# Projections by seven block products from the second group on, with weight operands fetched by ScalarE's queue

## The chip, the cores and the metric

One core of a Trainium2 chip runs the kernel. The metric is the device time in microseconds of one execution. Engine names are those of the profile: PE (TensorE), PEld (its weight loads), DVE (VectorE), ACT (ScalarE), POOL (GpSimd), and SP, whose queue issues every DMA of the kernel before.

## What is computed

The input x is 4 x 2048 x 512 (batch, rows, channels), in float32. The first half of the block is causal attention with one head of width 512; the second half, a gated sparse feed-forward layer, is not touched by the change.

```python
h = layernorm(x)
q = relu(h @ Wq + bq)
k = relu(h @ Wk + bk)
v = relu(h @ Wv + bv)
e = q @ k.T / sqrt(512) - 10000 * causal
attn = softmax(e)
x = x + layernorm(relu((attn @ v) @ Wo + bo))
x = x + layernorm(ffn(layernorm(x)))
```

## The kernel before, in words

**Precision.** Every float32 operand of an attention matmul is held as two float16 parts, high and low. A product is three matmuls (high by high, high by low, low by high), written by `three` (line 628), each with its own load of a 128 x 128 weight. The high part is an ACT activation, the low part a DVE or POOL subtraction after it.

**Stages.** The 8192 rows are 16 groups of 512 rows (g = 0 to 15), four groups to a batch; a group has four tiles of 128 rows. The attention phase runs over half steps H = 8g + h. `stages` (line 79) gives the half steps h = 0, 1 to v, 2, 3 to q, 4, 5 to k, each with two blocks of 128 output channels, and 6, 7 to v times Wo. `project` (line 642) makes one block: 4 channel chunks by 3 matmuls with 512 moving columns, so 48 matmuls for each of v, q and k of a group. Between them stands the attention of the group before: scores of a tile in h = 0, 2, 4 (and of the group's own first tile in h = 7), attention by values in h = 1, 3, 5, 6. `pe_items` (line 117) writes the order: in h = 0 and 1 the projection comes first, in the others attention does. A score tile at position t of its batch has t/4 + 1 chunks of up to 512 columns, so the attention work of a group grows fourfold along a batch. The group in which the attention of a batch begins (g = 1, 5, 9, 13; `opening`) is the shortest.

**Banks.** Six PSUM banks are one ring for projections, v times Wo and scores (`m_items`, line 278; `take_m`, line 635): a matmul group waits for the release of the bank six items before. Two more banks take attention by values.

**Evacuation.** `relu` (line 886, ACT) reads a finished block twice, as float32 `raw` and as the float16 high part; `lo_vqk` (line 1168, DVE) makes the low part. The order of each engine is written by hand in one loop over H per engine: SP line 557, PE 710, ACT 941, DVE 1355, POOL 1690. Each queue is strictly in order. What DVE does in an opening group, in its order:

- h = 0: low parts of v, residual statistics of an earlier tile, `score_rows` (line 1191), `convolution` (line 1270: one normalisation, two products, two reductions)
- h = 1: low parts of v and of the probabilities (`lo_p`), `convolution`, two `ln_stats` of the next group's rows (line 1156)
- h = 2: `score_rows`, low parts of q and probabilities, `bias_o` (line 1227), four `ln_norm` (line 1163)
- h = 3, 5: statistics or `convolution`, low parts, `bias_o`; h = 4: `score_rows`, low parts, statistics
- h = 6, 7: the low parts of v times Wo between the same kinds of work; two more `ln_stats` at the end of h = 7

**Rows of the next group.** SP loads them (`load_x`, line 457) at h = 5, two groups ahead; DVE normalises them in h = 2; ACT (`hi_h`, line 881) and POOL (`lo_h`, line 1648) split them in h = 3; SP transposes eight pieces of 128 x 512 by DMA into `hT`, double buffered (`transpose_h`, line 464).

**Start.** The four weight matrices are loaded into `w_stage` (line 381, the memory of v), split by `weight_hi` (line 871, ACT) and `weight_lo` (line 1144, DVE), and stay in SBUF for the whole phase. POOL's `ln_scale` (line 1638) waits for `ln_stats` of all four tiles of a group.

## Time and profile before

| | |
|---|---|
| median of 3 runs | 2062.92 us (2062.69 to 2063.83) |
| the profiled execution | 2062.52 us |
| its span | 2060.4 us |
| attention phase, in the trace | about 0 to 1390 us |
| granted clock of TensorE, mean | 0.998 |

The span is from the first to the last instruction of the program; the 2.1 us between it and the execution's time lie around it. In the page a busy share is that of the whole span. In a timeline the bracket holds the idle time of the engine before the row and who ended it. A row of a window gives the stretch, its length, then for PE, PEld, DVE, ACT and POOL the busy time and in brackets the instructions that run in it, then the granted clock, the DMA share and GB/s.

### The profile page before, as it was taken

The page shows a single profiled execution, that of the slowest core. Times are in us where ns is not written, and L with a number is a line of the kernel's source. Part 1 is how long each engine was busy: PE and PEld are TensorE (multiplying, and loading weights), DVE is VectorE, ACT ScalarE, POOL GpSimd, SP SyncE. Part 2 cuts the span into 40 slices and gives each one's busy share as a digit, 9 for nine tenths or more (in the row PEclk, how much of TensorE's full clock was granted, in tenths as well). Part 3 has the DMA queues.
Part 4 walks back from the last instruction along what each step waited for, and adds up shares of the span by engine and source line. Part 5 has one row for each costly group of instructions (what it writes and reads, how often), then busy time and mean ns, then how long its engine had stood idle before and what let it go on. Part 6 is the DMA issues. An engine that isn't in the chain of part 4 may idle for free. (4 is left out here: it accounts for less than half of the span.)

```text
span 2060.4 us, 30926 instructions
## 1 busy us (share of the span) xinstructions
PE 2002.2 (97%) x9419; PEld 937.9 (46%) x9419; DVE 1520.3 (74%) x3285; ACT 1101.9 (53%) x2268; POOL 1108.7 (54%) x1304
## 2 busy tenths in 40 slices
PE   8999999999999999999999999998999999999997
PEld 4444444444444444444444444453444444444443
DVE  6576554677555467565547765579999999999999
ACT  5444433344333434443334443335888888888885
POOL 2243322354323245333225432325999999999997
PEclk9999999999999999999999999999999999999999
DMA  5234342344342334423343332261222223223221
GB/s 185 75 92 112 73 99 73 99 110 110 86 102 76 78 90 125 102 77 95 78 94 97 110 88 66 88 179 63 80 96 93 88 87 98 94 96 97 89 78 67
DMA packets 301593, 194.85 MB, mean 95 GB/s; under 512 B 223858, under 2 KB 241394, under 8 KB 301428
## 3 DMA queue, kind: packets, MB, share of 16 engines
q1 hardware_dynamic: 301428, 192.88, 33.7%
q8 instruction: 75, 1.23, 0.3%
q14 instruction: 90, 0.74, 0.1%
HBM read 82.69 MB, written 58.72 MB: 69 GB/s over the span
## 5 line engine op out<-in xcount | busy, mean ns | idle before, releaser
L631 PE MATMUL psum<-hT,w_hi 128*128 128x512 f16 (+1 forms) x1544 | 458.3, 379 | 0.0
L631 PE MATMUL psum<-kT,qT 128*128 128x512 f16 (+3 forms) x1920 | 363.4, 347 | 1.5 <-DVE kT L1173 1.5
L631 PE MATMUL psum<-v,pT 128*128 128x512 f16 x1632 | 362.5, 379 | 0.7 <-DMA pT<-phl 0.7
L631 PE MATMUL psum<-hT,w_lo 128*128 128x512 f16 (+1 forms) x772 | 292.3, 379 | 0.0
L631 PEld LDWEIGHTS psum<-kT,qT 128*128 128x128 f16 x1920 | 180.9, 98 | 184.1 <-issue 2.9
L905 ACT ACTIVATE sS<-sS,nm 128x128 f32<-128x128 f32 (+7 forms) x64 | 76.9, 1201 | 345.9 <-DVE nm L1216 345.8
L894 ACT ACTIVATE raw<-psum,bqkv_s 128x512 f32<-128x512 f32 x192 | 131.2, 683 | 218.7 <-PE psum L631 216.5
L631 PEld LDWEIGHTS psum<-v,pT 128*128 128x128 f16 x1632 | 159.7, 98 | 193.1 <-issue 1.2
L1528 DVE MAX8 c<-cut 128x8 f32<-128x512 f32 x384 | 247.0, 691 | 0.0
L631 PEld LDWEIGHTS psum<-hT,w_hi 128*128 128x128 f16 x1544 | 151.5, 98 | 176.2 <-DVE w_lo L1147 0.3
L1655 POOL TENSOR_SCALAR ve<-mv 128x1 f32<-128x1 f32 x64 | 22.5, 352 | 348.2 <-DVE mv L1242 347.3
L631 PE MATMUL psum<-fw,xsT 128*128 128x512 f16 x768 | 176.2, 379 | 0.7 <-ACT xsT L1053 0.7
L631 PE MATMUL psum<-fw,h2T 128*128 128x512 f16 x768 | 176.5, 379 | 0.0
L1524 DVE MATCH_REPLACE8 cut<-c,cut 128x512 f32<-128x512 f32 x256 | 172.6, 688 | 0.0
L1730 POOL TENSOR_TENSOR sel<-ex,rest 128x512 f32<-128x512 f32 x126 | 160.7, 1275 | 11.6 <-DVE rest L1524 11.6
L1665 POOL TENSOR_TENSOR xr<-ob,xr 128x512 f32<-128x512 f32 x62 | 78.7, 1269 | 160.0 <-ACT ob L924 160.0
L631 PE MATMUL psum<-w_hi,vT 128*128 128x512 f16 x512 | 158.2, 379 | 0.0
L1205 DVE TENSOR_SCALAR_CACHE_REDUCE sS<-psum 128x512 f32<-128x512 f32 x96 | 66.0, 690 | 115.9 <-PE psum L631 115.6
L790 PE MATMUL psum<-lw,xa 128*128 128x512 f32 x252 | 142.7, 648 | 0.0
L1642 POOL TENSOR_SCALAR ve<-mv 128x4 f32<-128x4 f32 (+1 forms) x19 | 5.7, 302 | 228.4 <-DVE mv L1161 228.3
L1173 DVE TENSOR_TENSOR qT<-raw,qT 128x512 f16<-128x512 f32 x64 | 47.0, 735 | 102.3 <-ACT qT L895 102.3
L1178 DVE SCALAR_TENSOR_TENSOR v<-psum,v 128x512 f16<-128x512 f32 x64 | 44.0, 687 | 102.0 <-ACT v L900 102.0
(177 smaller groups left out, 3754.2 us busy)
## 6 DMA issues: line engine op xcount, KB each, us to landing
xg<-x SPq DMA_DIRECT2D x64, 256.0 KB, 5.1
xr<-x SPq DMA_DIRECT2D x64, 256.0 KB, 2.9
h_scratch<-hb SPq DMA_DIRECT2D x64, 256.0 KB, 3.0
h<-h_scratch SPq DMA_DIRECT2D x64, 256.0 KB, 2.7
x<-x_scratch SPq DMA_DIRECT2D x64, 256.0 KB, 3.0
x_scratch<-xr SPq DMA_DIRECT2D x62, 256.0 KB, 2.0
out<-zn SPq DMA_DIRECT2D x59, 256.0 KB, 2.0
xcg<-xc_scratch SPq DMA_DIRECT2D x16, 512.0 KB, 4.1
```

The source lines that it names most:

```text
L631: mm = nc.tensor.matmul(outp, stat(a), mov(c), start=(n == 0 and k == 0), stop=(n == total - 1 and k == 2))
L790: nc.tensor.matmul(L_BANK[s], xa[:, slot, j, s, :], lw[:, s, :], start=False, stop=True).then_inc(lg_ps.sem, 1)
L894: nc.scalar.activation(raw[:, n % 2, :], bank, ACT.Relu, bias=bias, scale=QKV_DOWN)
L905: nc.scalar.activation(sS[:, T % 2, 0:w], sS[:, T % 2, 0:w], ACT.Exp, bias=nm[:, T % 3:T % 3 + 1], accum_out=ssum[:, T % 3:T % 3 + 1]).the ...
L1173: nc.vector.tensor_tensor(dst[:, 1], raw[:, n % 2, :], dst[:, 0], ALU.subtract).then_inc(vqk_lo.sem, 1)
L1178: nc.vector.scalar_tensor_tensor(v[:, 1, T % TILES, :], m_bank(("vo", g, j)), V_DOWN, v[:, 0, T % TILES, :], ALU.mult, ALU.subtract).then_ ...
L1205: nc.vector.tensor_scalar(dst, src, S_SCALE, None, ALU.mult, ALU.max, accum_out=pm[:, T % 3, j:j + 1]).then_inc(s_ev.sem, 1)
L1524: nc.vector.match_replace(dst, eight, src, 0.0).then_inc(top_ok.sem, 1)
L1528: nc.vector.max(dst, src).then_inc(top_ok.sem, 1)
L1655: nc.gpsimd.tensor_scalar(ve2[:], m[:, 1:2], EPS * O_GAIN * O_GAIN, None, ALU.add).then_inc(ve2_ok.sem, 1)
L1665: nc.gpsimd.tensor_tensor(xr[:, T % 4, :], ob[:, T % 2, :], xr[:, T % 4, :], ALU.add).then_inc(x1_ok.sem, 1)
L1730: nc.gpsimd.tensor_tensor(sel[:, k % 2, s, :], ex[:, k % 4, s, :], rest[:, k % 2, s, :], ALU.subtract) \
```

## The change

Group 0 is projected as before. From g = 1 on each of v, q, k is made by Strassen's method: the 512 channels and the 512 rows are halved, the quarters of the weight matrix and of the rows are combined to seven pairs, and seven products of half size replace eight. One product is 2 output blocks by 2 channel chunks by 3 matmuls, 12 matmuls with 256 moving columns; v, q and k take 84 of these each. Products 0 to 3 run in the first half step of a projection, 4 to 6 in the second.

```diff
-            w_hi = sa("w_hi", [P, 4, C, D], F16)
-            w_lo = sa("w_lo", [P, 4, C, D], F16)
-            hT = sa("hT", [P, 2, 2, C, 512], F16)
+            ring = sa("ring", [P, QUARTERS, 2, 2, 256], F16)
+            w_o = sa("w_o", [P, 2, C, D], F16)
+            hT_early = sa("hT_early", [P, 2, 4, 2, 2, 256], F16)
+            hT_late = sa("hT_late", [P, 3, 2, 2, 256], F16)
...
+        A_BANK, C_BANK, B_BANK = M_BANK[0:3]
+        P_BANKS = (A_BANK, C_BANK, B_BANK, A_BANK, C_BANK, A_BANK, B_BANK)
+
+        m_items = [i for H in range(HALVES) for i in pe_items(H) if i[0] in ("s", "x") or (i[0] == "vo" and i[2] == C - 1)]
```

Scores and the fourth block of v times Wo now share a ring of three banks (`take_m` waits for the item three before); the products and the other blocks have the other three.

```diff
+                    if part_of == 0:
+                        arrived(0)
+                        vacated(0, (vqk_ev, COPY_U3), (vqk_lo, SUM_22))
+                        multiply(0, True)
+                        vacated(1, (vqk_lo, SUM_12))
+                        multiply(1, True)
+                        arrived(1)
+                        vacated(2, (vqk_lo, SUM_21))
+                        multiply(2, True)
+                        pe.wait_ge(vqk_ev.sem, vqk_ev.at(step_at(kind, g, COPY_1)))
+                        multiply(3, False)
+                    else:
+                        arrived(2)
+                        pe.wait_ge(vqk_ev.sem, vqk_ev.at(step_at(kind, g, COPY_5)))
+                        multiply(4, False)
+                        pe.wait_ge(vqk_ev.sem, vqk_ev.at(step_at(kind, g, COPY_U2)))
+                        multiply(5, False)
+                        arrived(3)
+                        pe.wait_ge(vqk_lo.sem, vqk_lo.at(step_at(kind, g, SUM_11)))
+                        multiply(6, True)
```

`arrived(n)` waits for weights and transposed rows by DMA. `vacated` names steps of the projection before (for v, the blocks of v times Wo). v times Wo in h = 6 waits for SUM_22, SUM_12, SUM_21 and COPY_U3 of k. The steps of one projection: ACT copies four partial sums out of PSUM into `part` (two activations of 256 columns each) and makes four high parts; DVE adds four products to them and makes four low parts.

```diff
+                    for m in range(2):
+                        a = nc.scalar.activation(part[:, n, 256 * m:256 * (m + 1)], P_BANKS[p][:, 256 * m:256 * (m + 1)], ACT.Identity,
...
+                    nc.vector.scalar_tensor_tensor(part[:, n, :], P_BANKS[p], sign * QKV_DOWN, part[:, n, :], ALU.mult, ALU.add) \
...
+                    nc.vector.scalar_tensor_tensor(dst[:, 1], in_two(n), 0.0, dst[:, 0], ALU.max, ALU.subtract).then_inc(vqk_lo.sem, 1)
```

ACT's order for h = 2 and 3 (4 and 5 the same), with the fetches of the next projection's weights in between; DVE's after it, h = 1, 2 and 3:

```diff
+                    elif h in (2, 4):
+                        if kind:
+                            copy_1(kind, g)
+                        exponential(s)
+                        if kind:
+                            copy_5(kind, g)
+                            refill(kind, g, 0)
+                        hi_p(s, first)
+                        if kind:
+                            hi_11(kind, g)
+                            copy_u2(kind, g)
+                            refill(kind, g, 1)
+                        hi_p(s, rest_of)
+                    elif h in (3, 5):
+                        if kind:
+                            hi_12(kind, g)
+                            copy_u3(kind, g)
+                            refill(kind, g, 2)
+                            hi_22(kind, g)
+                            hi_21(kind, g)
+                            refill(kind, g, 3)
...
+                            sum_12(kind, g)
+                            sum_22(kind, g)
+                        lo_p(early, first)
+                        if kind:
+                            lo_12(kind, g)
+                            sum_21(kind, g)
+                        lo_p(early, rest_of)
+                        if kind:
+                            lo_22(kind, g)
+                            lo_21(kind, g)
                         late(H, (3, convolution))
...
+                    elif h == 2:
+                        score_rows(s)
+                        if kind:
+                            sum_11(kind, g)
+                        late(H, (0, bias_o))
+                        lo_p(s, first)
+                        if kind:
+                            lo_11(kind, g)
+                        lo_p(s, rest_of)
...
+                    elif h in (3, 5):
+                        late(H, (3, convolution), (1, attention_stats), (2, residual_stats))
+                        if kind:
+                            sum_12(kind, g)
+                            sum_22(kind, g)
+                            lo_12(kind, g)
+                        late(H, (0, bias_o))
+                        if kind:
+                            sum_21(kind, g)
+                            lo_22(kind, g)
+                            lo_21(kind, g)
```

In h = 0 ACT does `copy_1`, `copy_5`, a refill, `hi_11`, `copy_u2`, a refill, `exponential`; DVE does `sum_11`, residual statistics, `lo_11`, `score_rows`, `convolution` and the next group's first two `ln_stats`, which stood in h = 7. `sum_12` waits for product 4; `hi_12` for `sum_12`; `copy_u3` stands behind `hi_12` on ACT; `sum_22` waits for `copy_u3`.

The combined weights are made once in group 0: four POOL operations on quarters per matrix (`mix`, at H = 0, 1, 3), an ACT and a DVE split (`mixed_hi`, `mixed_lo`, at H = 1, 2, 4), 14 stores of 128 KB per matrix to DRAM by SP (H = 1, 3, 5), then the first loads of the ring.

```diff
+                def mixed_hi(kind):
+
+                    act.wait_ge(mix_ok, 4 * (VQK.index(kind) + 1))
...
+                def first_ring():
+
+                    sp.wait_ge(wc_out, 32 * QUARTERS * len(VQK))
+                    for n, (a, b) in enumerate(((0, 2), (2, 4), (4, 6), (6, 7))):
+                        sp.dma_start(ring[:, a:b].rearrange("p q a c n -> p q (a c n)"), wc_d[0, :, a:b, :]).then_inc(w_in[n], 16)
...
+                        nc.scalar.dma_start(ring[:, a:b].rearrange("p q a c n -> p q (a c n)"), wc_d[run % len(VQK), :, a:b, :]) \
```

The next group's rows are split in quarters: POOL makes four differences and seven low parts (h = 3 to 6) where it made four low parts, ACT seven high parts for four, SP 14 transposes for eight (h = 4 to 7), and the load two groups ahead moves from h = 5 to the end of h = 7.

```diff
                     if h == 3 and g + 1 < NG:
-                        for j in range(GROUP):
-                            lo_h(g + 1, j)
+                        lo_h(g + 1, 0)
+                        lo_h(g + 1, 2)
+                        difference(g + 1, 2, (0, 0), (0, 1), (0, 0))
```

## Rows read from the trace of the kernel before

**Rows 1.** The page, busy time, share of the span, instructions.
```profile
PE 2002.2 (97%) x9419; PEld 937.9 (46%) x9419; DVE 1520.3 (74%) x3285; ACT 1101.9 (53%) x2268; POOL 1108.7 (54%) x1304
```

**Rows 2.** Waits of PE: waited for, us in total, times, longest.
```profile
PE psum L631 <- DVE kT L1173: 1.5, 2, 0.8
...
PE psum L631 <- DMA pT<-phl: 0.7, 1, 0.7
```

**Rows 3.** Timeline of PE, start and length in us, 12 to 62 us.
```profile
12.32 0.63 PE L631 MATMUL psum<-hT,w_hi 128*128 128x256 f16 x2
...
12.96 0.63 PE L631 MATMUL psum<-hT,w_hi 128*128 128x256 f16 x2
...
15.74 0.61 PE L631 MATMUL psum<-hT,w_hi 128*128 128x512 f16 x2
...
44.25 0.38 PE L631 MATMUL psum<-w_hi,vT 128*128 128x512 f16 x1
...
49.43 0.83 PE L631 MATMUL psum<-kT,qT 128*128 128x128 f16 x12
50.10 0.38 PE L631 MATMUL psum<-w_hi,vT 128*128 128x512 f16 x1
...
60.46 1.47 PE L631 MATMUL psum<-kT,qT 128*128 128x256 f16 x12
61.77 0.59 PE L631 MATMUL psum<-hT,w_hi 128*128 128x512 f16 x2
```

**Rows 4.** Windows of groups 1, 5, 6 and 8: busy us by engine.
```profile
55.28:112.73 57.45, 57.45 (x285) 27.47 (x284) 36.22 (x76) 29.02 (x53) 18.56 (x25) 1.00 0.36 90
...
397.77:455.75 57.98, 57.26 (x283) 26.96 (x282) 45.74 (x87) 27.95 (x51) 29.90 (x41) 1.00 0.43 103
455.75:533.49 77.74, 77.74 (x379) 36.47 (x378) 53.25 (x106) 34.04 (x59) 34.12 (x45) 1.00 0.38 104
...
631.96:740.78 108.82, 108.82 (x523) 50.57 (x522) 57.22 (x119) 37.40 (x63) 31.38 (x42) 1.00 0.35 89
```

**Rows 5.** Timeline of DVE in group 5, which starts at 397.77.
```profile
404.45 1.78 DVE L1173 TENSOR_TENSOR vT<-raw,vT 128x512 f16<-128x512 f32 x1 [0.46 <-ACT vT L895]
...
417.05 0.56 DVE L1208 CUSTOM_DVE_ANT_0 sS<-psum,mask_s 128x384 f32<-128x384 f32 x1
...
434.19 1.29 DVE L1173 TENSOR_TENSOR kT<-raw,kT 128x512 f16<-128x512 f32 x1 [4.14 <-ACT kT L895]
...
444.06 0.68 DVE L1247 BATCH_NORM_STATS2 st<-xr 128x6 f32<-128x512 f32 x1
```

**Rows 6.** Groups by line and form, weight loads: count, busy us, mean ns of one.
```profile
L631 PEld LDWEIGHTS psum<-kT,qT 128*128 128x128 f16 x1920 | 180.9, 98 | 184.1 <-issue 2.9
```

**Rows 7.** Groups by line and form: count, busy us, mean ns of one.
```profile
L1173 DVE TENSOR_TENSOR qT<-raw,qT 128x512 f16<-128x512 f32 x64 | 47.0, 735 | 102.3 <-ACT qT L895 102.3
...
L1234 DVE SCALAR_TENSOR_TENSOR ob<-psum,rcp,bo_b 128x512 f32<-128x512 f32 x64 | 48.0, 751 | 9.1 <-PE psum L631 2.7
...
L930 ACT ACTIVATE pilot<-psum 128x256 f32<-128x256 f32 x1 | 0.4, 362 | 0.0
...
L884 ACT ACTIVATE hhl<-xg 128x512 f16<-128x512 f32 x60 | 32.7, 619 | 0.0
...
L1650 POOL TENSOR_TENSOR hhl<-xg,hhl 128x512 f16<-128x512 f32 x60 | 69.8, 1197 | 3.5 <-ACT hhl L884 3.5
```

**Rows 8.** Timeline of SP's queue: length of the issues themselves.
```profile
42.39 2.00 SPq L462 DMA_DIRECT2D xg<-x  x4
44.44 5.13 SPq L469 DMA_TRANSPOSE hT<-hhl  x4
```

**Rows 9.** Timelines of ACT and of POOL in group 0.
```profile
24.88 1.91 ACT L874 ACTIVATE w_hi<-v 128x2048 f16<-128x2048 f32 x1
...
31.10 1.35 POOL L1645 TENSOR_TENSOR rs<-ve,expo 128x4 f32<-128x4 f32 x1
```

**Rows 10.** DMA issues of the page: count, KB each, us to landing.
```profile
v<-wqkvo SPq DMA_DIRECT2D x3, 1024.0 KB, 7.8
```

More of the change, by code:

```diff
@@ L289, in layer_block @@
         xg_in = [sig(f"xg_in{j}", 16) for j in range(GROUP)]
-        hT_in = [sig(f"hT_in{j}", 32) for j in range(GROUP)]
+        hT_in = [sig(f"hT_in{j}", step) for j, step in enumerate((64, 64, 64, 32))]
+        wc_out, mix_ok = sem("wc_out"), sem("mix_ok")
         pT_in = [sig(f"pT_in{j}", 32) for j in range(4)]
@@ L562, in _ @@
                         transpose_p(GROUP * (g - 1) + 3)
-                    if h == 5 and opening(g):
+                    if h == 5 and g + 1 < NG:
                         transpose_h(g + 1, 1)
@@ new lines, in _ @@
+                        hi_p(early, first)
+                        if kind:
+                            hi_22(kind, g)
+                            hi_21(kind, g)
+                            refill(kind, g, 3)
+                        hi_p(early, rest_of)
+                    elif h in (2, 4):
+                        if kind:
+                            copy_1(kind, g)
+                        exponential(s)
+                        if kind:
+                            copy_5(kind, g)
+                            refill(kind, g, 0)
+                        hi_p(s, first)
+                        if kind:
+                            hi_11(kind, g)
+                            copy_u2(kind, g)
+                            refill(kind, g, 1)
+                        hi_p(s, rest_of)
+                    elif h in (3, 5):
+                        if kind:
+                            hi_12(kind, g)
+                            copy_u3(kind, g)
+                            refill(kind, g, 2)
+                            hi_22(kind, g)
+                            hi_21(kind, g)
+                            refill(kind, g, 3)
+                    elif h == 7:
+                        exponential(s)
+                        for n, span in ((0, first), (1, rest_of)):
+                            hi_vo(*st[n][1:])
+                            hi_p(s, span)
@@ L981, in _ @@
                         normed(due(H, 1))
-                    if h == 3 and g + 1 < NG:
-                        for j in range(GROUP):
-                            hi_h(g + 1, j)
+                    if 3 <= h < 7 and g + 1 < NG:
+                        hi_h(g + 1, *((0, 2), (1,), (3,), (4, 5, 6))[h - 3])
                     if due(H, 4) == 0:
@@ L1368, in _ @@
                         early = s_tile(H - 1)
-                        for n, part in ((0, first), (1, rest_of)):
-                            if st:
-                                lo_vqk(*st[n])
-                            if early is not None:
-                                lo_p(early, part)
-                        late(H, (3, convolution))
-                        if g + 1 < NG:
+                        if kind:
+                            sum_12(kind, g)
+                            sum_22(kind, g)
@@ L1376, in _ @@
+                    if H == 0:
+                        weight_lo(3)
+                    if H == 1:
+                        weight_lo(4)
+                    if H in (1, 2, 4):
+                        mixed_lo(VQK[H // 2])
+                    if g + 1 < NG:
+                        if h == 0:
+                            ln_stats(g + 1, 0)
+                            ln_stats(g + 1, 1)
+                        if h == 1:
                             ln_stats(g + 1, 2)
                             ln_stats(g + 1, 3)
-                    elif h == 2:
-                        if s is not None:
-                            score_rows(s)
-                        if st:
-                            lo_vqk(*st[0])
-                        late(H, (0, bias_o))
-                        if s is not None:
-                            lo_p(s, first)
-                        if st:
-                            lo_vqk(*st[1])
-                        if s is not None:
-                            lo_p(s, rest_of)
-                        if g + 1 < NG:
+                        if h == 2:
```

428 lines of the change are left out of this document (285 added, 143 removed).

## The prediction

> **What bounds the kernel now.** The page first: PE is busy for 97% of the span, DVE for 74%, ACT and POOL for little over half [rows 1]. Then the waits of PE: in the attention phase it stands still three times after the start, 2.2 us in all [rows 2]. Then how fast it goes. From 15.74 to 44.25 us lie 132 matmuls of 512 columns, 216.0 ns each; twelve of 256 columns take 61.77 - 60.46 = 1.31 us, 109.2 ns each; twelve of 128 take 0.67 us, 55.8 ns each [rows 3]. So the attention phase is a stream of matmuls, and a matmul less is time less, as long as nobody makes PE wait.
>
> Whether somebody will is read from the windows by group. A late group of a batch has room: group 8 takes 108.8 us with DVE busy for 57.2. The opening group 5 takes 58.0 us with DVE busy for 45.7; group 6 has 53.3 of 77.7; group 1, with no tiles behind it, 36.2 of 57.5 [rows 4]. In group 5 DVE has no idle bracket between 404.45 and 417.05, where it takes up the scores of h = 2 [rows 5]. That is 19.3 us into the group. DVE is late there, and the six-bank ring hides it.
>
> **The change, part by part.**
>
> *The gain.* A projection before is 48 x 216.0 = 10.37 us. After, it is 84 x 109.2 = 9.17 us. The difference, 1.20 us, comes 45 times (three in each of 15 groups): **-53.8 us**, or 3.6 us a group.
>
> Does a matmul of half the columns still hide its weight load? A load takes 98 ns [rows 6], yet matmuls of 128 columns follow each other at 55.8 ns [rows 3], so it is hidden far below 109 ns. The Trainium skill (TensorE: Matmul & The Clock Gate, Back-to-back issue gap) gives for a stream of load and matmul pairs about 81 ns at 128 columns and 131 at 512. By a line between these, an estimate from that page, 256 columns would take 98 ns, a projection 8.2 us against 6.3, and the change would cost 87 us. The rows contradict both of its ends (55.8 and 216.0), and the sum goes by the rows.
>
> *The new work beside PE.* For each projection DVE has four sums and four low parts where it had four low parts. A sum is nearest to the `ob` row (751 ns), a low part to the `qT` row (735) [rows 7]; back to back they start some 0.65 us apart. That is 2.6 us more a projection, 7.8 a group. ACT exchanges eight activations of 512 columns for eight of 256 (362 ns alone) and four of 619 ns [rows 7]: no more work. It also issues 12 refills a group, at SP's 0.5 us each [rows 8], and three more high parts: 8 us on top of 28. POOL makes seven more pieces of 1.2 us [rows 7], 8.4 us on top of 30. SP issues six more transposes at 5.13 / 4 = 1.28 us, 7.7 us a group. In long groups all of this lies beside PE. In group 5, shrunk to 54.4 us, DVE would need 45.7 + 7.8 = 53.5.
>
> *The new waits.* Before, PE needed DVE only six items later. Now the first product of q cannot start before `sum_22` of v, which waits for `copy_u3`, which stands behind `hi_12` on ACT, which waits for `sum_12`: some 1.4 us in which DVE stands, three times a group. And product 4 needs `copy_5`, which stands behind `exponential`, which waits for `score_rows`, which stands behind all that DVE had before. I laid out group 5, in us from its first product. PE without waits: h = 0 ends at 6.55, h = 1 at 11.15, h = 2 at 18.35, product 4 of q is wanted at 19.7, h = 3 ends at 23.5, h = 5 at 37.2, h = 7 at 54.4.
>
> - v: `sum_11` at 4.2, score rows to 7.4, `convolution` to 11, `ln_stats` to 12.9, `sum_12` 13.6, then `hi_12` and `copy_u3`, `sum_22` at 15.6. PE wants the bank at 13.1: 2.5 us.
> - q: DVE ends h = 1 (two low parts of probabilities and v, `sum_21`, two low parts, `convolution`, `ln_stats`) at about 24, score rows 24.8, exponential 25.7, `copy_5` 26.3. PE: 4 to 4.5 us more.
> - k: the same chain with `ln_norm` (2.5 us) and statistics before it; PE waits 1.5 for `sum_22` of q and 2 to 3 for `copy_1`, as ACT has four high parts, two activations of `ob` and two refills ahead of it.
> - v times Wo: its first block now waits for `sum_22` of k. DVE has `convolution` and residual statistics first. In the trace these end at 444.74, 47.0 us into the group [rows 5], and `sum_12`, the 1.4 us and `sum_22` come after, with the work added to h = 1 and 3 before them. The trace has one idle stretch of 4.1 us in front that can absorb part [rows 5]. PE wants the bank at 37.2 and 10 us of waits already taken, and gets it at 53 to 57: 6 to 7 us.
>
> Together 14 to 19 us; I take 16.5 for each of groups 5, 9, 13: **+50 us**. Group 1 lacks two `convolution`s in h = 0 and 1 (7 us) but not what stands before `sum_22` of k: 6 to 14 us, **+10.5**. Groups 2, 6, 10, 14, laid out the same way, wait 1.9, 1.6 and 1.8 us for `copy_5`, `copy_u2` and `copy_1`: 0 to 8, taken at 4, **+16**. In groups 4, 8, 12 the fourth score chunk of h = 2 needs a bank of the ring of three that DVE frees 1 to 3 us late: **+6**. Groups 3, 7, 11, 15 have room for it: their product 4 comes 6 us after `copy_5`.
>
> *The start.* POOL's four operations on a matrix take 4 x 1.2 and the steps between, 5.4 us. Those of q stand behind `ln_scale` of group 1, which waits for `ln_stats`, now behind the split of v's mixture on DVE (2.3 us). `ln_scale` ended at 32.45 [rows 9]; now at about 36, so q's mixture is there at 41.4. ACT stands in `mixed_hi` until then and reads the third block of q only by 44.7. The second block of k, which PE wants at 36.5, needs that bank: 8.2 us. `mixed_hi` (1.9 us [rows 9]) and `mixed_lo` of k then stand in front of k's last two blocks, and v times Wo waits for their low parts: it starts at 57.1 instead of 44.25 [rows 3]. With 10.5 us of v times Wo and scores PE is ready for group 1 at 68.2. SP must store k's mixture (14 issues at 0.5 us from about 59.5, landed at 68), load the ring (1 MB took 7.8 us [rows 10], the first 512 KB some 4) and transpose: product 2 starts at about 76, which puts the group at 74 where it stood at 55.3: **+19 us**, between 12 (the mixture hidden, the ring not) and 25.
>
> *The clock.* After each long stand PE may run slowly. The first projection matmuls after the start are 12.96 - 12.32 = 0.64 us for three, 213 ns for 256 columns, the 1.2 GHz level where the later ones take 109 [rows 3]. That stretch cost about 1.4 us. Nine stands over 4 us would be between 0 and 12.6; most of the new waits are DVE's, which do not lengthen with it: **+5**.
>
> *At nothing* I cost the refills (5.4 MB a group beside a DMA share of 0.34 to 0.43 [rows 4], each pair asked for 13 us before its use) and the later row loads, which land some 8 us into the next group while DVE wants them at 11. If refills slowed every transposition, PE would pay it at each half step; that is a rival below. The feed-forward phase does not change.
>
> **The sum.** Against the profiled execution's 2062.52 us (0.4 under the median): -53.8 + 50 + 10.5 + 16 + 6 + 19 + 5 = +52.7, so **2115 us**.
>
> **The rivals.**
>
> *The waits fit into idle time.* DVE has 12.2 us idle in group 5 and its work after is 53.5 in 54.4 us; my layout is made of mean durations, and ops overlap by up to 0.1 us at their ends. If DVE reaches the score rows of h = 2 so early that `copy_5` is there at 19.7 us, that is if they start by about 18, PE never waits. Then only the start is left: 2062.5 - 53.8 + 19 = 2028 us. Against it: they started at 19.3 before any work was added [rows 5]. Chance 0.16, with all up to 2068.
>
> *DMA decides.* The refills (some 82 MB more) land late or hold the transposes up. One us at each of 45 projections beyond the sum is 2160; if POOL also locks DVE out longer (a low part took 1.78 us once where the mean is 0.735 [rows 5, 7]), 2175. For it: every queue works more. Against: the shortest lead of a refill is 13 us. Chance 0.10.
>
> *Short matmuls paced by their loads.* If half of a 98 ns load showed, a matmul would take 158 ns and a projection 13.3 us: +2.9 x 45 = +131, with the start 2213 us. The 55.8 ns row speaks against it. The page of the Trainium skill named above speaks for it. Chance 0.01.
>
> That the change does not do what it says is ruled out by its counts: 84 matmuls of half size are issued.
>
> **The numbers.** The forecast has 0.73, its own range 2068 to 2158: the low ends give -53.8 + 12 + 6 + 3 x 14 = +6, the high ones -53.8 + 25 + 14 + 3 x 19 + 4 x 8 + 9 + 13 = +96. The range that leaves 2 in 10 out is 2055 to 2165; of the first rival 0.13 lies below it, of the second 0.06 above. A measurement of this kernel can tell 0.2%, 4.1 us, from no change. Faster by more: 0.13; within: 0.04; slower by more: 0.83.
>
> **What the profile after would show.** Right: matmuls of 256 columns 109 ns apart; long groups 3.6 us shorter; groups 5, 9, 13 at 67 to 74 us with PE waiting for `part` of ACT and DVE and DVE busy for over 50; group 1 starting near 74 us. Wrong: PE without waits in group 5, or DVE's score rows of h = 2 starting before 18 us; group 1 starting under 67; PE waiting for the ring or hT in later groups.

## The result, and the profile after

The changed kernel takes 2277.81 us (median of 4 runs, 2271.61 to 2280.59), the one before 2063.38 (4 runs). The ratio is 1.1035, with an interval of 1.1012 to 1.1058. Forecast were 2115 us and a range up to 2165: the direction is right, the size far off. The profiled execution spans 2269.8 us where the one before spans 2060.4, so +209.4 us are to be found.

The page of the changed kernel first, busy time by engine and the granted clock of TensorE in 40 slices:

```profile
PE 2020.0 (89%) x11039; PEld 1110.8 (49%) x11039; DVE 1691.3 (75%) x3468; ACT 1147.4 (51%) x2496; POOL 1261.8 (56%) x1421
...
PEclk9999999989999998899999889999999999999999
```

PE was busy for 97% of the span [rows 1] and is for 89%. Its busy time is even larger although the matmuls hold less work: a busy PE at half speed counts as busy. The clock row shows it, with 8s where before there were only 9s.

Then what PE and DVE wait for (waited for, us in total, times, longest):

```profile
PE psum L746 <- ACT part L1063: 44.2, 30, 2.8
PE psum L746 <- DVE part L1417: 38.2, 9, 8.4
PE psum L726 <- DVE part L1417: 34.7, 5, 8.5
PE psum L746 <- issue: 26.2, 12, 4.8
```

```profile
DVE dsq L1542 <- DMA xc_scratch<-dsq: 106.4, 16, 10.5
DVE part L1417 <- ACT part L1063: 104.1, 61, 4.4
```

Before the change PE had two such rows of 1.5 and 0.7 us [rows 2]. The row "issue" names nobody, but the trace does: each of these 12 stands, 26.2 us in all, ends 0.09 us after a transposed piece of `hT_late` has landed. PE waited there for SP's transposes directly. The row at the top of DVE's list, 106.4 us in 16 waits, was a small one before:

```profile
DVE dsq L1267 <- DMA xc_scratch<-dsq: 7.0, 3, 3.7
```

`dsq` has two buffers, so the convolution of a tile writes where the rows of the tile two before lie, and waits until SP has stored those.

The windows of groups 1, 5, 6 and 8 (start and end, length, busy us of PE, PEld, DVE, ACT, POOL, granted clock, DMA share, GB/s), to be laid beside [rows 4]:

```profile
76.30:150.50 74.20, 57.73 (x394) 38.85 (x393) 47.40 (x90) 33.22 (x73) 26.35 (x32) 0.93 0.65 159
...
459.30:548.10 88.80, 62.06 (x392) 39.89 (x391) 57.94 (x104) 32.28 (x68) 42.52 (x53) 0.87 0.56 144
548.10:639.90 91.80, 79.54 (x487) 48.03 (x486) 62.52 (x115) 35.99 (x71) 41.19 (x50) 0.94 0.62 152
...
741.60:855.70 114.10, 107.71 (x631) 61.66 (x630) 66.14 (x129) 40.13 (x78) 36.20 (x46) 0.97 0.57 136
```

Group 1 starts at 76.3 (forecast: 74). Group 5 takes 88.8 us for 58.0, group 6 91.8 for 77.7, and even group 8, which I had at 107, takes 114.1 for 108.8. DVE is busy for 57.9 us of group 5's 88.8, so it isn't full; it waits.

The matmuls do what was forecast. Timeline of PE, start and length in us, with a stand of PE in brackets:

```profile
711.06 4.09 PE L746 MATMUL psum<-hT_late,ring 128*128 128x256 f16 x36
714.99 1.24 PE L726 MATMUL psum<-v,pT 128*128 128x512 f16 x5
```

36 matmuls in 714.99 - 711.06 = 3.93 us are 109 ns each. The same view in group 5:

```profile
465.96 2.43 PE L746 MATMUL psum<-hT_early,ring 128*128 128x256 f16 x12 [2.62 <-ACT part L1063]
...
474.69 1.47 PE L746 MATMUL psum<-hT_late,ring 128*128 128x256 f16 x12 [1.65 <-issue]
...
487.15 5.02 PE L746 MATMUL psum<-hT_early,ring 128*128 128x256 f16 x31 [8.40 <-DVE part L1417]
```

After a stand of 2.62 us twelve matmuls take 2.43 us, after one of 1.65 us they take 1.47. In the first set the matmuls follow each other at 213 ns from the fifth on, the 1.2 GHz level (the granted clock of that stretch is 0.50). And the stand of 8.40 us leads back to DVE in the same stretch:

```profile
471.76 0.69 DVE L1538 TENSOR_TENSOR prod<-hb,cw_b 128x512 f32<-128x512 f32 x1
480.03 0.69 DVE L1542 TENSOR_REDUCE dsq<-prod 128x128 f32<-128x512 f32 x1 [7.58 <-DMA xc_scratch<-dsq]
```

DVE stands for 7.58 us between the two halves of one convolution, with `sum_12` and `sum_22` behind it. What it waits for is in SP's queue (start, length of the issues, count):

```profile
460.75 5.88 SPq L542 DMA_TRANSPOSE hT_late<-hhl  x4
466.68 0.58 SPq L580 DMA_DIRECT2D x_scratch<-xr  x1
467.30 0.60 SPq L588 DMA_DIRECT2D h_scratch<-hb  x1
468.00 2.40 SPq L570 DMA_TRANSPOSE pT<-rows  x2
470.50 2.60 SPq L542 DMA_TRANSPOSE hT_late<-hhl  x2
473.15 2.00 SPq L530 DMA_DIRECT2D xg<-x  x4
475.19 0.43 SPq L580 DMA_DIRECT2D x_scratch<-xr  x1
475.67 0.43 SPq L593 DMA_DIRECT2D xc_scratch<-dsq  x1
```

and the same store in the kernel before, whose group 5 starts at 397.77:

```profile
402.90 0.43 SPq L501 DMA_DIRECT2D xc_scratch<-dsq  x1
```

Before, the store goes out 5.1 us into the group; after, 16.4 us into it. Ahead of it stand the transposes of hT, those of the probabilities, and the four row loads that the change moved to the end of h = 7. They begin late, because SP had first stood for POOL's later parts, up to 460.75:

```profile
SPq L539 <- POOL hhl L1929: 13.2, 1, 13.2
```

So the lateness has two parts. The first transpose comes 1.5 us into the group, and from it to the store SP needs 14.9 us. The store also takes longer to land, 4.2 us in the median where it was 2.0.

**The balance.** From the PE records of groups 0 to 15 I added up, per group, gaps between matmuls of over 60 ns, and the extra time of matmuls that take twice their usual spacing. The three kinds of loss:

```
                                forecast    after    one plain copy   three edits on it
group 0, against before            +19      +20.9        +20.6            +18.4
waits, groups 5, 9, 13              50       80.8         77.8             51.3
waits, group 1                      10.5     17.3         15.6             10.1
waits, groups 2, 6, 10, 14          16       51.4         35.6              7.8
waits, groups 4, 8, 12               6       19.8          4.2              1.4
waits, groups 3, 7, 11, 15           0       19.6         12.0             11.7
half speed, groups 1 to 15           5       52.4         21.9             20.6
```

The last two columns are experiments below. Matmul work at full speed fell by 51.0 us (forecast 53.8). The column "after" adds to 262.2 - 51.0 = 211 us, against 209.4 of the spans. Waits of groups 1 to 15 were forecast at 82.5 us and are 188.9, so 106 us are unforeseen, and so are 47 us of half speed.

**DVE's work.** DVE is busy for 171 us more (1691.3 for 1520.3), where the prediction has 7.8 x 15 = 117, and for 57.9 us in group 5 where it has 53.5. The largest unforeseen item is the products of the convolution, which the change doesn't touch, before and after:

```profile
L1263 DVE TENSOR_TENSOR prod<-hb,cw_b 128x512 f32<-128x512 f32 x120 | 83.1, 692 | 8.3
L1538 DVE TENSOR_TENSOR prod<-hb,cw_b 128x512 f32<-128x512 f32 x120 | 111.9, 933 | 8.3
```

Of the 120, 56 took 1.21 us on average, and each of them had a two-operand operation of POOL beside it; the other 64 took 0.69 us and had none. The rival "DMA decides" names this ("if POOL also locks DVE out longer"). What part of PE's waits comes from it no run shows, as all variants below have it.

### The profile page after: what moved, and what is told of

Same layout as the page of the kernel before. It is cut to its first block and busy times, and to the rows that moved or that the text cites. A ratio compares the mean times of both kernels' runs of the same rounds, so it can differ in the third digit from the quotient of the medians.

```text
span 2269.8 us, 35462 instructions
## 1 busy us (share of the span) xinstructions
PE 2020.0 (89%) x11039; PEld 1110.8 (49%) x11039; DVE 1691.3 (75%) x3468; ACT 1147.4 (51%) x2496; POOL 1261.8 (56%) x1421
## 3 DMA queue, kind: packets, MB, share of 16 engines
q10 hardware_dynamic: 25344, 80.75, 13.8%
## 5 line engine op out<-in xcount | busy, mean ns | idle before, releaser
L726 PE MATMUL psum<-v,pT 128*128 128x512 f16 x1632 | 370.6, 385 | 10.6 <-DMA pT<-rows 10.4
L746 PE MATMUL psum<-hT_early,ring 128*128 128x256 f16 x2160 | 266.5, 285 | 66.1 <-DVE part L1417 38.2
L746 PEld LDWEIGHTS psum<-hT_early,ring 128*128 128x128 f16 x2160 | 217.7, 102 | 117.8 <-issue 49.6
L1417 DVE SCALAR_TENSOR_TENSOR part<-psum,part 128x512 f32<-128x512 f32 x180 | 124.1, 689 | 158.9 <-ACT part L1063 104.1
L746 PE MATMUL psum<-hT_late,ring 128*128 128x256 f16 x1620 | 194.0, 278 | 47.1 <-issue 26.2
L726 PE MATMUL psum<-w_o,vT 128*128 128x512 f16 x768 | 182.3, 396 | 42.2 <-DVE part L1417 34.7
L746 PEld LDWEIGHTS psum<-hT_late,ring 128*128 128x128 f16 x1620 | 158.6, 99 | 82.0 <-issue 50.1
L1063 ACT ACTIVATE part<-psum,bqkv_s 128x256 f32<-128x256 f32 x360 | 147.2, 466 | 78.8 <-PE psum L746 78.3
L1929 POOL TENSOR_TENSOR hhl<-xg,hhl 128x512 f16<-128x512 f32 x105 | 128.0, 1236 | 99.2 <-ACT hhl L1046 99.2
L1114 ACT ACTIVATE rows<-rows,nm 128x128 f32<-128x128 f32 (+7 forms) x64 | 76.7, 1199 | 197.2 <-DVE nm L1491 197.1
L1542 DVE TENSOR_REDUCE dsq<-prod 128x128 f32<-128x512 f32 x120 | 82.3, 686 | 110.0 <-DMA xc_scratch<-dsq 106.4
```

Of the source, the lines that this page charges most:

```text
L726: mm = nc.tensor.matmul(outp, stat(a), mov(c), start=(n == 0 and k == 0), stop=(n == total - 1 and k == 2))
L746: mm = nc.tensor.matmul(P_BANKS[p][:, 256 * m:256 * (m + 1)], ring[:, p, a, c, P * m:P * (m + 1)], h[:, b, c, :], start=(first and m + c + ...
L1063: a = nc.scalar.activation(part[:, n, 256 * m:256 * (m + 1)], P_BANKS[p][:, 256 * m:256 * (m + 1)], ACT.Identity, bias=bqkv_s[:, "qkv".ind ...
L1114: nc.scalar.activation(sS[:, T % 2, 0:w], sS[:, T % 2, 0:w], ACT.Exp, bias=nm[:, T % 3:T % 3 + 1], accum_out=ssum[:, T % 3:T % 3 + 1]).the ...
L1417: nc.vector.scalar_tensor_tensor(part[:, n, :], P_BANKS[p], sign * QKV_DOWN, part[:, n, :], ALU.mult, ALU.add) \
L1542: nc.vector.tensor_reduce(dsq[:, T % 2, 0, P * r:P * (r + 1)], prod[:].rearrange("p (g f) -> p g f", f=4), AX.X, ALU.add).then_inc(xc_ok.s ...
```

## The experiments

All runs were set beside the kernel before on the same chip (2062.66 to 2064.59 us). They come from three chips, and most variants have two executions, up to 7 us apart, so that differences below some 5 us between variants say little. Five questions: SP's queue (theory A), the round trip of the products' banks through ACT and DVE (B), the refills' traffic (C), the clock behind stands (D), DVE's own time (E).

**The stand-in.** Eleven of these kernels can't be compared with the true pair directly: each transposing transfer is replaced by plain copies from SBUF to SBUF on the same queue, so that rows and probabilities are not transposed and outputs differ. With three copies per transfer the queue is loaded more than by the true transfer (six copies, which stand for two transfers, took 3.71 us of it, two transposes 2.40 to 2.60), with one copy less. A plain copy also lands sooner (2.1 us in the median for pieces of `hT`; 2.4 us for `hT_late` and 4.0 for `hT_early` with true transposes), so a variant alters both.

```diff
+                def turn(dst, src, sem):
+                    for a, b in ((0, 48), (48, 96), (96, 128)):
+                        sp.dma_start(dst[a:b], src[a:b].rearrange("p (c n) -> p c n", n=P)).then_inc(sem, 16)
...
-                            sp.dma_start_transpose(dst.rearrange("p c (t n) -> p (c t) n", t=2), hhl[:, q % 4, a, :]) \
-                                .then_inc(hT_in[(0, 0, 1, 1, 2, 2, 3)[q]].sem, 16)
+                            turn(dst.rearrange("p c (t n) -> p (c t) n", t=2), hhl[:, q % 4, a, :], hT_in[(0, 0, 1, 1, 2, 2, 3)[q]].sem)
```

### Three plain copies, the kernel before and the changed one

> The kernel before with a stand-in for every DMA transpose: three plain SBUF to SBUF copies of the same bytes (48, 48 and 32 partitions), so the rows and the probabilities are not transposed. Three issues at 0.33 to 0.45 us take about what one transpose's issue took (1.28 us). Every theory: PE is as busy as before, 2060 to 2075 us. If it is far slower, plain copies are no fair stand-in.

> The changed kernel with the same stand-in (rows and probabilities not transposed). If the stand-in is fair, it stands to the one above as the changed kernel to the kernel before: 190 to 235 us longer, with DVE waiting about 100 us for the stores of the convolution rows, 200 us of waits of PE and some 58 us lost at half speed.

Before: 2089.29 us, ratio 1.0127 (1.0098 to 1.0157). After: 2402.47, ratio 1.1645 (1.1611 to 1.1679). Under this load the change costs 313 us where it cost 214. Both times miss their expectations (2060 to 2075, and 190 to 235 us between the two), so three copies overstate the queue and serve to show a direction, not a size. DVE's waits, first of the kernel before, then of the changed one, and a row of PE's:

```profile
DVE dsq L1270 <- DMA xc_scratch<-dsq: 25.5, 11, 7.4
```

```profile
DVE dsq L1544 <- DMA xc_scratch<-dsq: 209.1, 16, 15.9
DVE part L1419 <- ACT part L1065: 99.9, 59, 4.4
```

```profile
PE psum L748 <- issue: 102.4, 18, 8.5
```

The wait for the convolution's stores doubles from 106.4 to 209.1 us when each of SP's transfers takes more issues; the wait for ACT stays (104.1 to 99.9). PE's direct wait for transposed rows grows from 26.2 to 102.4 us, and its wait for the probabilities' from 10.4 to 36.1. In the kernel before the store's wait goes from 7.0 to 25.5 us. So these waits grow with the length of the queue, with the seven products and without them.

### One plain copy

```diff
-                    for a, b in ((0, 48), (48, 96), (96, 128)):
+                    for a, b in ((0, 128),):
```

> The changed kernel with one plain copy for every DMA transpose (rows and probabilities not transposed): SP's issues of a transpose shrink from about 1.28 to 0.45 us, some 14 us of SP's queue a group in groups 1, 5, 9, 13 and 30 in the long ones. Theory A (SP's queue comes late to the stores, DVE stands before the reduction of h = 0, PE pays): 40 to 110 us faster than with three copies. Theory B (DVE's own work and its exchange with ACT set the pace): under 20 us faster.

> Control for the run of the changed kernel with one plain copy in the place of each transposing transfer (2199.0 us). The kernel before, with the same stand-in (probabilities and rows are copied, not transposed, so the results differ). Theory A (the change's loss comes from SP's queue, which holds more work ahead of the convolution's stores): here the convolution's wait stays under 20 us in all, the time is 2045 to 2065 us, and the change costs 135 to 155 us under this stand-in, of 214 us with the true transfers. Rival (the stand-in only makes everything faster): the time is 60 us or more below 2063, and the change's own cost is unchanged at 190 us or more.

The changed kernel takes 2199.0 us (ratio 1.0659, 1.0615 to 1.0702), 203 us less than with three copies, far more than the 40 to 110 expected. The kernel before takes 2063.78 us in the same form (ratio 0.9995, 0.9983 to 1.0006): it had room in SP's queue and gains nothing from more. The change costs 135 us here. SP's queue and DVE's waits in the changed one:

```profile
437.88 3.00 SPq L527 DMA_DIRECT2D hT_late<-hhl  x4
...
442.12 1.12 SPq L527 DMA_DIRECT2D pT<-rows  x2
443.34 1.22 SPq L527 DMA_DIRECT2D hT_late<-hhl  x2
444.60 2.05 SPq L534 DMA_DIRECT2D xg<-x  x4
```

```profile
DVE part L1419 <- ACT part L1065: 106.8, 62, 4.4
...
DVE dsq L1544 <- DMA xc_scratch<-dsq: 36.6, 9, 6.3
```

A transfer's issue is 0.56 to 0.75 us here, where transposes took 1.20 to 1.47. Theory A stands: 79 of the 214 us go with the time that SP's transfers take, and the store's wait falls from 106.4 to 36.6 us. The rival (the stand-in makes everything faster) falls with the control. But the theory named one path only. PE's direct waits for transposed rows and probabilities, 26.2 and 10.4 us with the true transposes, are gone too. And the opening groups 5, 9 and 13 gain only 3.3 to 3.8 us each. In group 5 the store now goes out 11.0 us into the group, still too late: DVE waits 6.3 us for it, and the stand before q's first product stays.

```profile
461.37 7.63 PE L748 MATMUL psum<-hT_early,ring 128*128 128x256 f16 x48 [8.94 <-DVE part L1419]
```

### The store one half step earlier

```diff
-                    for lag, move in ((-1, load_residual), (2, store_x1), (4, store_h2), (6, store_xc)):
+                    for lag, move in ((-1, load_residual), (2, store_x1), (4, store_h2), (5, store_xc)):
```

With three copies:

> The changed kernel with the stand-in of three copies, and one edit: SP stores the convolution rows one half step earlier, ahead of the probabilities' transposes, the last hT transposes and the four row loads of h = 7. Theory A: DVE's wait for these stores falls from about 106 us to under 20, and the time falls by 60 to 110 us. Theory B: the wait falls but others grow by as much, and the time falls by less than 25 us.

2323.67 us (ratio 1.1263, 1.1230 to 1.1296), 79 us less than 2402.47. The store's wait falls from 209.1 to 9.1 us, and another stands in its place:

```profile
DVE st L1399 <- DMA xg<-x: 101.0, 16, 8.8
```

The queue is still as long, and now the row loads are what comes late. An earlier place for one transfer moves the wait to the next one. With one copy the queue is short enough to profit:

> The changed kernel with one plain copy per transfer (2199.0 us), and SP stores the convolution's rows one half step earlier. Theory A (what is left of the wait of 36.6 us is SP's order): the wait falls under 8 us and the time falls by 10 to 30 us. Rival (with SP's queue short, the wait hides beside the waits for ScalarE, or goes over to the row loads): within 6 us of 2199.

2167.98 us (ratio 1.0504, 1.0473 to 1.0534): 31 us less than 2199.0, just over the forecast, and neither a store's nor a load's wait is left among DVE's large ones. The stand before q's first product in group 5 falls from 8.94 to 2.33 us, which ties it to the store:

```profile
453.97 7.07 PE L747 MATMUL psum<-hT_early,ring 128*128 128x256 f16 x48 [2.33 <-DVE part L1418]
```

### The round trip

```diff
-COPY_1, COPY_5, HI_11, COPY_U2, HI_12, COPY_U3, HI_22, HI_21 = range(8)
+COPY_1, COPY_5, HI_11, COPY_U2, COPY_U3, HI_12, HI_22, HI_21 = range(8)
...
-                            hi_12(kind, g)
                             copy_u3(kind, g)
+                            hi_12(kind, g)
```

> The changed kernel with one plain copy per transfer (2199.0 us), and in all 45 projections ScalarE copies u3 out of its bank before it rounds the last block of q, k, v to bf16, so that VectorE's last combination (which waits for it) can start earlier. Theory B (what is left of the loss is the round trip of the products' banks, PE to ScalarE to VectorE and back to PE): VectorE's wait for ScalarE (106.8 us in 62 waits) falls by a third or more, and the time falls by 20 to 45 us, to 2154 to 2179. Rival (the copy is late because ScalarE is busy with the other work of the stage, not with the order of these two): within 10 us of 2199.

(The rounded parts are float16; "bf16" in the expectation is a slip.) 2165.62 us (ratio 1.0486, 1.0456 to 1.0516), 33 us less. DVE's waits:

```profile
DVE part L1419 <- ACT part L1065: 41.6, 22, 4.4
```

The wait fell from 106.8 us in 62 waits to 41.6 in 22: forty times DVE no longer stands while ACT rounds a block. This was the step "some 1.4 us in which DVE stands, three times a group" of the prediction, and its cost was the order of two operations on ACT. Theory B stands.

### The refills' traffic

```diff
-                        nc.scalar.dma_start(ring[:, a:b].rearrange("p q a c n -> p q (a c n)"), wc_d[run % len(VQK), :, a:b, :]) \
+                        nc.scalar.dma_start(ring[:, a:b].rearrange("p q a c n -> p q (a c n)")[:, :, 0:256], wc_d[run % len(VQK), :, a:b, 0:256]) \
```

Three quarters of each operand keep the first run's weights, so later groups are computed with other weights.

> The changed kernel with one plain copy per transfer (2199.0 us), and every refill of a weight operand brings only a quarter of its bytes (the rest keeps what lay there, so the products of later groups use other weights). The issues and their number stay. Theory C (the DMA engines' traffic of the refills delays rows, stores and transfers): over 40 us faster. Rival (traffic is cheap at a DMA share below 15%, what costs is the place in the queues): within 15 us of 2199.

2184.63 us (ratio 1.0578, 1.0547 to 1.0609), 14 us less for 60 MB less (queue 10 moved 20.20 MB instead of 80.75), at the edge of what the rival allowed. The traffic counts for something, as the store's wait goes from 36.6 to 22.8 us, but it is not the cause.

### The clock

PE alone runs 21 bursts of 96 matmuls of 512 columns, and between two bursts waits for 1, 2, 3, 4, 6, 8 or 12 operations of DVE, three times over (the third round ends before its wait for 12). The attention isn't computed.

```diff
+                for n in range(len(GAPS)):
+                    if n:
+                        pe.wait_ge(gap, n)
+                    for k in range(96):
+                        mm = nc.tensor.matmul(ps[:, k % 2, :], h[:, 0:P], h[:], start=True, stop=True, skip_group_check=True)
+                    mm.then_inc(burst, 1)
```

> The clock by itself: nothing of the layer is computed. 21 bursts of 96 matmuls of 512 columns (20.7 us each), between them PE waits for 1, 2, 3, 4, 6, 8 or 12 DVE operations of 512 columns, three times over (about 0.9 to 8.5 us). Theory D (what cost the changed kernel 58 us at half speed is the stands themselves, short ones too): bursts after stands of 2.5 to 4 us begin at 427 ns a matmul for about 3 us at least once in three, and every burst after the longest stands does, at 1.3 to 2.9 us each. Rival (as forecast: only stands over 4 us, 1.4 us each): the short stands leave every burst at 216 ns.

Timeline of PE, start and length of the bursts with the stand in brackets:

```profile
50.49 20.89 PE L40 MATMUL ps<-h 128*128 128x512 f16 x96 [1.38 <-DVE t L53]
73.36 22.58 PE L40 MATMUL ps<-h 128*128 128x512 f16 x96 [1.98 <-DVE t L53]
98.52 20.89 PE L40 MATMUL ps<-h 128*128 128x512 f16 x96 [2.58 <-DVE t L53]
123.19 23.53 PE L40 MATMUL ps<-h 128*128 128x512 f16 x96 [3.77 <-DVE t L53]
151.69 22.94 PE L40 MATMUL ps<-h 128*128 128x512 f16 x96 [4.97 <-DVE t L53]
181.99 23.15 PE L40 MATMUL ps<-h 128*128 128x512 f16 x96 [7.36 <-DVE t L53]
```

A burst at full speed takes 20.89 us. After 3.77 to 7.36 us it takes 2.0 to 2.6 us more, after 1.98 us 1.7 more, and after 2.58 us nothing more; the rounds agree. So the price of a stand doesn't grow evenly with its length, and a stand of 2 us can carry it already. What decides is open: the rounds repeat the same sequence 177.7 and 177.5 us apart, so that length and place in time were never varied apart, and that 2.58 us cost nothing where 1.98 us did speaks against length alone. The prediction had charged 1.4 us, and only stands over 4 us.

In the changed kernel, with one copy, 30 matmuls were then put into each opening group's two long waits (group 1: the second alone), into a bank that nothing reads:

```diff
+                def fill(item, n):
+                    bank = take_m(item)
+                    for c in range(n):
+                        nc.tensor.matmul(bank, w_o[:, 0, 0, 0:P], w_o[:, 0, c % C, :], start=True, stop=True, skip_group_check=True)
```

> The changed kernel with one plain copy per transfer (2199.0 us), and 30 extra matmuls of 256 columns into a free bank of the ring ahead of the two long waits of each opening group (values and q's products), whose results nothing reads. Each set is 30 x 109 ns = 3.3 us of work, in waits of 8 us. Theory D (a stand of PE of over 2 us costs a half-speed stretch behind it, some 2.3 us each, and work in the stand avoids it): half-speed extra falls from 28.4 us to 15 us or less, and the time falls by 5 to 16 us. Rival (the fillers only shorten the stand, which is still long enough to drop the clock, or end after what was waited for): the same within 5 us, or later by up to 10 us.

(The matmuls have 512 columns, not 256 as the expectation says: a set is 6.5 us.) The time is 2196.07 us (ratio 1.0633, 1.0603 to 1.0664), 2.9 us less than 2199.0; the executions of the two overlap, so this is no difference. The rows before `v` times Wo, first with one copy, then with the fillers:

```profile
503.39 4.50 PE L728 MATMUL psum<-w_o,vT 128*128 128x512 f16 x12 [8.49 <-DVE part L1419]
```

```profile
494.77 6.64 PE L806 MATMUL psum<-w_o 128*128 128x512 f16 x30
503.30 2.76 PE L728 MATMUL psum<-w_o,vT 128*128 128x512 f16 x12 [1.89 <-DVE part L1429]
```

At the spot itself it works: twelve matmuls take 2.76 us instead of 4.50. But the half-speed time of groups 0 to 15 stays (27.6 us, now 27.1): other stretches appear, most of them behind stands of 2.0 to 3 us. Theory D's forecast of 15 us or less fails and the rival holds: fillers don't win the loss back here. That DVE sets the end of a group in either case would explain it, and is argued, not tested.

### DVE's own time

```diff
-                    nc.vector.scalar_tensor_tensor(part[:, n, :], P_BANKS[p], sign * QKV_DOWN, part[:, n, :], ALU.mult, ALU.add) \
+                    nc.vector.scalar_tensor_tensor(part[:, n, 0:64], P_BANKS[p][:, 0:64], sign * QKV_DOWN, part[:, n, 0:64], ALU.mult, ALU.add) \
```

> The changed kernel with one plain copy per transfer (2199.0 us), and each of VectorE's 180 combinations of the products handles 64 of its 512 columns (the others keep the first copy alone, so q, k and v differ). Its rows stand at 689 ns; 64 columns are taken as about 0.15 us, so 97 us of VectorE's work go, about 6.5 us in each projection's stage. Theory E (VectorE's own time in the chain of combinations is what is left, above all in the opening groups): the opening groups fall from 84.5 us to 78 or less and the time by 30 us or more. Rival (the chain goes by ScalarE and the waits, VectorE has room): less than 12 us faster.

2166.55 us (ratio 1.0497, 1.0466 to 1.0527), 32 us less. The combinations' row:

```profile
L1419 DVE SCALAR_TENSOR_TENSOR part<-psum,part 128x64 f32<-128x64 f32 x180 | 40.1, 223 | 172.2 <-ACT part L1065 106.7 <-PE psum L748 65.5
```

84 us of DVE's work are gone (124.1 to 40.1) and the kernel is 32 us shorter, while DVE's waits for ACT stay at 106.7. The total meets theory E, but the opening groups fall from some 84.5 us to 80.6 to 82.5, not to 78. DVE's own time is one part of the chain, of the size of the round trip.

### All three edits together

One copy, `copy_u3` first, the store a half step earlier, and on POOL in group 0:

```diff
+                    if H == 1:
+                        mix("q")
                     if h == 1 and g + 1 < NG:
                         ln_scale(g + 1, 0, GROUP)
...
-                    if H in (0, 1, 3):
+                    if H in (0, 3):
```

> The changed kernel with one plain copy per transfer (2199.0 us) and three edits: ScalarE copies u3 first (alone 2165.6 us), SP stores the convolution's rows one half step earlier (wait of 36.6 us for them), and GpSimd mixes q's rows ahead of its ln_scale in the opening groups. Theory A plus B (the waits are independent and add): the convolution's wait falls under 8 us and the time to 2125 to 2150 us. Rival (the store moved earlier only makes the row loads late, and the opening groups are bound by the chain of four combinations): 2155 to 2166 us. In neither does it beat the kernel before (2064).

2130.66 us (ratio 1.0323, 1.0282 to 1.0364), 68 us less than 2199.0 where 31 and 33 alone and 2 in group 0 give 66: the waits are independent and add. (The expectation speaks of the opening groups; the order on POOL changes group 0 only, which ends at 73.5 us for 75.7.) Windows of groups 5 and 6:

```profile
420.80:496.80 76.00, 59.61 (x393) 39.12 (x391) 57.98 (x102) 32.41 (x69) 41.89 (x52) 0.91 0.54 169
496.80:573.00 76.20, 74.69 (x488) 46.78 (x487) 62.22 (x115) 35.86 (x72) 38.84 (x48) 1.00 0.58 181
```

Group 6 is now at 76.2 us, below the 77.7 of before, and the long groups 7 and 8 are at 97.8 and 105.5 for 98.5 and 108.8. Only the opening groups still lose 18 us each, group 1 9 us and the start 18. It doesn't beat the kernel before. A version in which the opening groups keep eight products, so that the mixtures also have time, is what these numbers point to; it was not tried, nor were the edits with true transposes.

## Why the prediction was wrong

**Right.** The gain (51.0 us, forecast 53.8) and the spacing of 109 ns, by which the page of the Trainium skill (TensorE: Matmul & The Clock Gate, Back-to-back issue gap) is contradicted again: its 81 ns at 128 columns and 131 at 512 stand against 56 and 216 ns, the median spacings in the changed kernel. The start: group 1 at 76.3 us for 74, with two stands of 7.5 us for the banks of k and of `v` times Wo. Most of PE's waits in the opening groups, in kind: for `sum_22` of v, q and k and for `copy_5` of q. The rival that waits fit into idle time is dead, as is the one of matmuls paced by their loads.

**The step that failed first** is "*At nothing* I cost the refills ... and the later row loads", with "SP issues six more transposes ... In long groups all of this lies beside PE". I added up SP's work and asked whether it fitted into the group; I never asked who stands behind it in the queue. SP works in order. Six more transposes that wait for POOL, and four loads moved to h = 7, push back the store of the convolution's rows by 11 us, and DVE waits for it with two buffers: 106.4 us in 16 waits, of which none stood in my layout of group 5. There `convolution` was laid at its working time. The stand before q's first product I had at 2.5 us (PE wants the bank at 13.1 and gets it at 15.6); it was 8.40. With a short queue and the store moved it was 2.33. The same lateness reached PE directly too: 26.2 us for pieces of `hT_late` and 10.4 for the probabilities. The prediction had named that as a sign of being wrong ("PE waiting for the ring or hT in later groups"), and it came. In groups 2, 6, 10, 14 I had 16 us for all four and there were 51.4. With the true transposes the store's share is argued and not shown; the stand-ins bracket it (1.0659 and 1.1645 around 1.1035).

**What the layout lacked besides the queue.** With one copy and the store moved, and everything else in the order that I had laid out, the waits of groups 5, 9, 13 are still 64 us for 50, of group 1 15 for 10.5, of groups 2, 6, 10, 14 21 for 16, and the time is 2167.98. In group 5 the layout has nothing for v's fourth product, which stood 2.6 us for `copy_1` in every variant, and 6 to 7 us before `v` times Wo, where 8.5 were measured. So the 51.3 us of the three edits against the forecast's 50, and their 2130.66 beside its 2115, are luck in part: those edits took out of the kernel the round trip that the layout had priced. I also added 57.1 and 10.5 to 68.2, which should be 67.6; nothing hangs on it.

**The second** is "*The clock*": 5 us, with a price of 1.4 us for nine stands over 4 us. There were 31 half-speed stretches of 1.0 to 2.9 us, 52.4 us of them in groups 1 to 15. Both factors were too small: measured alone a stand that cost anything cost 1.7 to 2.6 us, and in the kernel stands of under 3 us already did. My argument that the waits "are DVE's, which do not lengthen with it" may be wrong in kind as well, since a slow stretch delays the products for which ACT and DVE then wait; no run separates that.

**The rival "DMA decides"** (2160 to 2175) was nearest in time and had the right witness, "every queue works more", but for its reason, the refills' traffic, `small_refill` gives 14 us of some 135. Its clause "hold the transposes up" was nearer: PE did wait for transposes, though for their place in the queue more than for the traffic. I had named the shortest lead of a refill as the argument against; the lead of a store was the one to look for. Also not in the sum: the long groups, where I had "room for it", wait 19.6 us in 3, 7, 11 and 15.

## What to carry to other kernels

When a change adds issues to an in-order DMA queue, list each later transfer of that queue with the buffer that it frees and its lead, as one does for an engine: a share of busy time says nothing here, since the store that came late took 0.43 us itself. List the engines that wait for the queue directly as well: here PE's own waits for it were 36.6 us. A wait that the view puts down to "issue" is worth a look at what landed just before its end. Fewer operations on PE pay only where the engines behind it have slack per bank: with the three edits and one copy the longer groups won 0.7 to 3.3 us each, and opening ones still lost 18. When a simpler variant meets a forecast, ask whether it still holds what the forecast had priced. Where a combination waits for a copy on another engine, put that copy ahead of any rounding; that was 33 us for the order of two operations.

## What the runs showed of the hardware

- A stand of PE of 1.98 us put 1.7 us of half-speed time behind it each of three times, one of 2.58 us none, those of 3.77 to 7.36 us 2.0 to 2.6 us. In the changed kernel half-speed stretches began behind stands of 2.3 us and more, behind all 14 of over 4 us after the start, and not behind each shorter one. Filling 6.6 of 8.5 us with matmuls ended it at that spot.
- The issue of a transposing transfer occupied SP's queue for 1.20 to 1.47 us, that of a plain copy of the same tiles 0.56 to 0.75 us, and of a store of the convolution's rows 0.43 us.
- Products of the convolution on DVE (two operands, 512 columns) took 0.69 us, and 1.21 us where POOL ran a two-operand operation beside them: 56 of 120 in the changed kernel, none before.
- A combination on DVE took 689 ns with 512 columns and 223 ns with 64, so cutting the width eightfold leaves a third of the time.
